# Router and experts of an adaLN block in plain float32 products instead of three-part bf16 ones; shared experts by feature rows, expert tiles written out, rows gathered by the index list in place

## The reference

```python
sa, ca, ga, sb, cb, gb = (silu(c) @ wmod) in six parts      # ga, gb pushed away from 0
h = layernorm(x) * (1 + ca) + sa
x = x + ga * attention(h)                                   # window of 8, softmax
h = layernorm(x) * (1 + cb) + sb
scores = sigmoid(h @ gate_w.T)                              # 2048 rows x 16 experts
topv, topi = top_k(scores, 2);  topv = topv / topv.sum()
y = mlp(h, sw1, sw2, sw3)                                   # shared, 352 wide
for e in range(16):                                         # 176 wide
    y = y + mlp(h, w1[e], w2[e], w3[e]) * weight of e for each row
x = x + gb * y
# mlp(x) = (silu(x @ w1.T) * (x @ w3.T)) @ w2.T; expert weights are bf16, h is float32
```

## Time and profile before

| | |
|---|---|
| median of 3 runs | 536.55 us (536.25 to 541.13) |
| profiled execution | 534.09 us |
| its span, first to last instruction | 532.3 us |
| mean granted TensorE clock | 0.914 |
| busy: TensorE, weight loads | 389.3 us (73%), 285.3 us (54%) |
| busy: VectorE, ScalarE, GpSimd | 311.2, 156.6, 169.8 us |
| chain that ended last | PE 52%, DVE 16%, issue 11%, unknown queue 8% |

### The profile page before, as it was taken

The page is one execution under the profiler, slowest core; times in us unless marked ns, Lnnn a source line. Parts: engine busy times, 40 slices in busy tenths (PEclk is TensorE's granted clock), DMA queues, the critical chain, the costliest instruction groups (busy, mean ns, idle before and its releaser), DMA issues.

```text
span 532.3 us, 14579 instructions
## 1 busy us (share of the span) xinstructions
PE 389.3 (73%) x5617; PEld 285.3 (54%) x5618; DVE 311.2 (58%) x704; ACT 156.6 (29%) x348; POOL 169.8 (32%) x164
## 2 busy tenths in 40 slices
PE   2779899998989898864877877765766576579200
PEld 0448687777868787643555655443544354346100
DVE  4736667775847575733979954444444445345283
ACT  1202041323222232214333223333333323334240
POOL 6100041222212230421000024545645555554362
PEclk9969999999999999986999989899898989987755
DMA  8440432314040314007300022222222322231392
GB/s 303 141 109 24 99 105 52 119 43 140 19 137 14 113 44 135 23 13 272 84 1 1 1 60 70 77 66 82 75 72 81 91 68 75 85 84 45 93 301 79
DMA packets 42313, 46.48 MB, mean 87 GB/s; under 512 B 21519, under 2 KB 36536, under 8 KB 42049
## 3 DMA queue, kind: packets, MB, share of 16 engines
q1 hardware_dynamic: 35491, 30.12, 18.7%
q0 software_dynamic: 5376, 13.65, 8.9%
q10 hardware_dynamic: 1398, 2.00, 1.1%
HBM read 32.03 MB, written 13.71 MB: 86 GB/s over the span
## 4 chain that ended last, share of the span: by engine, by line
PE 52%; DVE 16%; issue 11%; another core or an unknown queue 8%; ACT 4%; POOL 2%; DMA 2%; SPq 1%; DVEq 1%; POOLq 0%; ACTq 0%
PE bank L1246 9%; PE bank L1045 6%; PE bank L1072 6%; PE bank L1007 5%; PE bank L1054 3%; PE bank L1258 3%; PE bank L1060 2%; DVE second_region L927 2%; PE bank L1024 2%; PE bank L1159 2%; DVE hid L888 2%; PE bank L1089 2%; PE bank L1037 2%; ACT second_region L566 2%
## 5 line engine op out<-in xcount | busy, mean ns | idle before, releaser
L439 POOL DMA_INDIRECT second_region<-hrows,ixg x48 | 47.4, 989 | 139.0 <-DVE ixg L932 66.8
L1246 PE MATMUL bank<-region,second_region 128*128 x288 | 56.7, 337 | 25.5 <-DVE second_region L927 22.9
L888 DVE TENSOR_TENSOR hid<-second_region,bank 128x176 f32<-128x176 f32 (+1 forms) x64 | 24.4, 382 | 75.3 <-ACT second_region L566 62.2
L448 POOL DMA_INDIRECT yrows<-yo,ixp x48 | 50.8, 1059 | 19.6 <-issue 12.6
L1246 PEld LDWEIGHTS bank<-region,second_region 128*128 128x128 bf16 x288 | 27.4, 103 | 47.6 <-issue 36.2
L566 ACT ACTIVATE second_region<-bank 128x176 f32<-128x176 f32 (+1 forms) x64 | 22.5, 353 | 99.7 <-PE bank L1246 56.3
L1152 PE MATMUL bank<-cft,hid 128*88 128x128 f32 (+1 forms) x144 | 30.0, 304 | 29.7 <-DVE hid L888 28.4
L1258 PE MATMUL bank<-region,hT 88*128 x288 | 43.4, 291 | 1.1 <-DVE hT L902 1.0
L701 DVE RECIPROCAL second_region<-bank 128x256 f32<-128x256 f32 x16 | 28.1, 1758 | 26.2 <-PE bank L1077 26.2
L1045 PE MATMUL bank<-region,second_region 64*32 64x128 f32 x1024 | 38.4, 287 | 4.1 <-issue 4.1
L397 POOL TENSOR_TENSOR rstd2s<-ve,cft 128x2 f32<-128x2 f32 x8 | 5.5, 692 | 104.8 <-DVE ve L724 104.8
(11 more groups left out here) (150 smaller groups left out, 738.7 us busy)
## 6 DMA issues: line engine op xcount, KB each, us to landing
region<-vd SPq DMA_DIRECT2D x32, 128.0 KB, 3.2
modb<-moddram SPq DMA_DIRECT2D x8, 512.0 KB, 4.5
region<-yrows SPq DMA_DIRECT2D x16, 256.0 KB, 5.5
hrows<-h SPq DMA_DIRECT2D x8, 384.0 KB, 2.5
region<-w13T SPq DMA_DIRECT2D x1, 2816.0 KB
region<-second_region SPq DMA_DIRECT2D x64, 32.0 KB, 1.8
vd<-second_region SPq DMA_DIRECT2D x8, 256.0 KB, 2.2
out<-xs SPq DMA_DIRECT2D x8, 256.0 KB, 2.1
```

The source lines that it names most:

```text
L439: gp.indirect_dma_start(rows[:, j, :], None, hrows, bass.IndirectOffsetOnAxis(ap=ixg[:, j:j + 1], axis=0)).then_inc(fetch[j], 16)
L448: gp.indirect_dma_start(yrows, bass.IndirectOffsetOnAxis(ap=ixp[:, j:j + 1], axis=0), yo[:, j, :], None, bounds_check=TOPK * T - 1, oob_is ...
L888: dve.tensor_tensor(hid[:, j % 2, 0:w], act_s[:, j % 2, 0:w], bank[j % 2][:, boff:boff + w], ALU.mult).then_inc(hid_s, 1)
L1246: last = pe.matmul(bank[j % 2][:, 0:2 * I], rT[:, j % 2, q, :], w13[:, q % C, bass.ds(e, 1), :], start=q == 0, stop=q == PARTS * C - 1)
```

## The change

The products of router, shared experts and experts take float32 operands instead of three bf16 parts. h stays one float32 tile hx; hrows holds it in 1024 bytes a row. `modulated` on GpSimd is what is left of `split`; `turn_h` has 4 float32 transposes and `gate` 4 float32 products; ScalarE's `gate_exp` reads the scores from PSUM. In the tiles, hid's transposes are copied once (`turned_hidden`, to hT2), and `up` has 2, `down` 2 products, `turn_rows` 2 transposes.

The shared experts work on groups of four row tiles with the hidden features on the partitions: `up_shared` makes for 12 blocks (4 groups of 3) two products pairs of 512 columns, so that hid needs no transpose, and `down_shared` has 3 products a tile. The routing runs first for the 14 tiles that are ready, then for the last two (`rank` twice), and stands in another order between the shared blocks.

The weights must be float32 in SBUF: GpSimd loads sw13, sw2 and w2 at the start with a widening transfer; w13 is loaded in bf16 to a staging place, its first part in batch row 1 of the attention, and widened by eight copies on ScalarE (`widen`).

The 48 tiles are written out on all engines, with waits on constants; the transfers read their column of sloti directly, and ixg, ixp are gone. The buffers of the tiles lie where those of the shared experts lay, so the gathers wait for the last shared product (sy_p). The steps are in another order: `up` runs two tiles ahead (three PSUM places), `turn_rows` three; GpSimd's scatter is that of tile s, and stands behind the gather of s + 4.

The diff, cut to the tiles, the shared experts and the gate:

```diff
-            def split(b):
+            def modulated(b):
 
                 wait(gp, l2_xn, b + 1)
                 wait(gp, mod_ld, 16 * (b + 1))
                 gp.tensor_tensor(h2[:, :, :], h2[:, :, :],
-                                 modb[:, b, 2 * D:3 * D].unsqueeze(1).to_broadcast([P, U, D]), ALU.mult).then_inc(l2_mu, 1)
+                                 modb[:, b % 2, 2 * D:3 * D].unsqueeze(1).to_broadcast([P, U, D]), ALU.mult).then_inc(l2_mu, 1)
                 wait(gp, l2_mu, b + 1)
-                gp.tensor_tensor(h2[:, :, :], h2[:, :, :],
-                                 modb[:, b, D:2 * D].unsqueeze(1).to_broadcast([P, U, D]), ALU.add).then_inc(l2_h, 1)
-                wait(gp, p_hi, b + 1)
-                gp.tensor_tensor(hr[:, :, :], h2[:, :, :], h3[:, :, 0], ALU.subtract).then_inc(p_r, 1)
-
-            def last_part(b):
-                wait(gp, p_mid, b + 1)
...
-            gp.wait_ge(routed, 1)
-
-            def get(s, j, i):
+            gp.wait_ge(who_s, 2)
+            gp.wait_ge(sy_p, TT)
+
+            def get(s):
 
                 wait(gp, rT_p, s - RING + 1)
-                settle(gp)
-                wait(gp, ixg_s, s + 1)
-                settle(gp)
-                gp.indirect_dma_start(rows[:, j, :], None, hrows,
-                                      bass.IndirectOffsetOnAxis(ap=ixg[:, j:j + 1], axis=0)).then_inc(fetch[j], 16)
-
-            def give(s, j, i):
+                gp.indirect_dma_start(rows[:, s % RING, :], None, hrows,
+                                      bass.IndirectOffsetOnAxis(ap=sloti[:, 0, s:s + 1], axis=0)).then_inc(fetch[s % RING], 16)
+
+            def give(s):
 
                 wait(gp, yo_s, s + 1)
-                settle(gp)
-                wait(gp, ixp_s, s + 1)
-                settle(gp)
-                gp.indirect_dma_start(yrows, bass.IndirectOffsetOnAxis(ap=ixp[:, j:j + 1], axis=0),
-                                      yo[:, j, :], None, bounds_check=TOPK * T - 1,
-                                      oob_is_err=False).then_inc(put[j], 16)
-
-            def step(s, j, i):
-                if not (isinstance(s, int) and s + AHEAD >= NS):
-                    get(*later(i, j, AHEAD))
-                if not (isinstance(s, int) and s < 2):
-                    give(*later(i, j, -2))
-
-            for s in range(AHEAD):
-                get(s, s, 0)
-            over_tiles(gp, step, NS, RING)
-            for s in (NS - 2, NS - 1):
-                give(s, s % RING, s // RING)
+                gp.indirect_dma_start(yrows, bass.IndirectOffsetOnAxis(ap=sloti[:, 1, s:s + 1], axis=0),
+                                      yo[:, s % RING, :], None, bounds_check=TOPK * T - 1,
+                                      oob_is_err=False).then_inc(put[s % RING], 16)
+
+            for s in range(RING):
+                get(s)
+            for s in range(NS):
+                if s + RING < NS:
+                    get(s + RING)
+                give(s)
 
...
+            def silu(s):
+                wait(act, up_p, s + 1)
+                wait(act, hid_s, s - 1)
+                act.activation(act_s[:, s % 2, :], UP(s)[:, 0:I], ACT.Silu).then_inc(silu_s, 1)
+
+            def turned_hidden(s):
+                wait(act, ht_p, s + 1)
+                wait(act, y_p, s - 1)
+                act.activation(hT2[0:IH, s % 2], HT(s), ACT.Copy).then_inc(ht_s, 1)
+
+            def result(s):
+                wait(act, y_p, s + 1)
+                wait(act, put[s % RING], 16 * (s // RING))
+                act.activation(yo[:, s % RING, :], YP(s), ACT.Copy).then_inc(yo_s, 1)
+
+            silu(0)
+            silu(1)
+            for s in range(NS):
+                turned_hidden(s)
+                if s + 2 < NS:
+                    silu(s + 2)
+                if s > 0:
+                    result(s - 1)
+            result(NS - 1)
 
             for b in range(B):
                 act.wait_ge(ld_y[b], 16 * TOPK)
@@ -671,13 +665,6 @@
             for i, k in enumerate((2, 5)):
...
             def gate(b):
                 wait(pe, xT_s, b + 1)
                 if b == 0:
-                    pe.wait_ge(gw_s, 2 * PARTS - 1)
+                    pe.wait_ge(ld_g, 16)
                 for u in range(U):
-                    for q in range(PARTS * C):
-                        last = pe.matmul(LG[u], xT[:, U * b + u, q, :], gw3[:, q % C].rearrange("p k e -> p (k e)"),
-                                         start=q == 0, stop=q == PARTS * C - 1)
+                    t = U * b + u
+                    for c in range(C):
+                        last = pe.matmul(LG[:, u], xT[:, c, t * P:(t + 1) * P], gws[:, c, :], start=c == 0, stop=c == C - 1)
                 last.then_inc(lg_p, 1)
 
...
+            def up_shared(n):
+                g, f = divmod(n, SK)
+                p = SI - (SK - 1) * P if f == SK - 1 else P
+                wait(pe, su_m, n - 1)
+                for half, o in enumerate((SA(n), SB(n))):
+                    for c in range(C):
+                        last = pe.matmul(o[0:p], sw13[:, c, half * SI + f * P:half * SI + f * P + p],
+                                         xT[:, c, g * GT * P:(g + 1) * GT * P], start=c == 0, stop=c == C - 1)
+                last.then_inc(su_p, 1)
+
+            def down_shared(g):
+                wait(pe, su_m, SK * (g + 1))
+                for i in range(GT):
+                    wait(pe, sy_s, GT * g + i - 1)
+                    for f in range(SK):
+                        p = SI - (SK - 1) * P if f == SK - 1 else P
+                        last = pe.matmul(YP(i), hid_g[0:p, g % 2, f, i * P:(i + 1) * P], sw2[0:p, f, :],
+                                         start=f == 0, stop=f == SK - 1)
+                    last.then_inc(sy_p, 1)
+
+            def rank(a, z):
+
...
-            def turn_rows(s, j, i):
-                wait(pe, fetch[j], 16 * (i + 1))
-                wait(pe, rT_s, s - 1)
-                if isinstance(s, int) and s < 2:
-                    pe.wait_ge(hid_s, TT)
-                for q in range(PARTS * C):
-                    last = pe.transpose(RTP(j)[:, q * P:(q + 1) * P], rows[:, j, q * P:(q + 1) * P], identb)
+            down_shared(0)
+            up_shared(6)
+            down_shared(1)
+            up_shared(7)
+            up_shared(8)
+            sitters()
+            up_shared(9)
+            down_shared(2)
+            up_shared(10)
+            up_shared(11)
+            down_shared(3)
+
+            def turn_rows(s):
+                wait(pe, fetch[s % RING], 16 * (s // RING + 1))
+                wait(pe, rT_s, s)
+                for c in range(C):
+                    last = pe.transpose(RTP[:, c * P:(c + 1) * P], rows[:, s % RING, c * P:(c + 1) * P], ident)
                 last.then_inc(rT_p, 1)
 
-
-            held = [pe.alloc_register(f"expert_of_tile{k}") for k in range(RING + 2)]
-            experts = [None] * (RING + 2)
+            held = [pe.alloc_register(f"expert_of_tile{k}") for k in range(RING)]
+            later = [pe.alloc_register(f"expert_of_late_tile{k}") for k in range(RING)]
...
-            def down(s, j, e):
-                wait(pe, lo_s, TT + s + 1)
-                if isinstance(s, int) and s < 2:
-                    pe.wait_ge(y_s, TT + s - 1)
-                else:
-                    wait(pe, yo_s, s - 1)
+            def turn_hidden(s):
+                wait(pe, hid_s, s + 1)
+                wait(pe, ht_s, s - 1)
                 for k in range(2):
-                    for q in range(PARTS):
-                        last = pe.matmul(YP(j), hT3[0:IH, j % 2, q, k, :], w2[:, k, bass.ds(e, 1), :],
-                                         start=k == 0 and q == 0, stop=k == 1 and q == PARTS - 1)
+                    last = pe.transpose(HT(s)[:, k, :], hid[:, s % 2, k * IH:(k + 1) * IH], ident)
+                last.then_inc(ht_p, 1)
+
+            def down(s):
+                wait(pe, ht_s, s + 1)
+                wait(pe, yo_s, s - 1)
+                for k in range(2):
+                    last = pe.matmul(YP(s), hT2[0:IH, s % 2, k, :], w2[:, k, bass.ds(experts[s], 1), :],
+                                     start=k == 0, stop=k == 1)
                 last.then_inc(y_p, 1)
 
-            def step(s, j, i):
-                if j == 0 and not (isinstance(s, int) and s == 0):
-                    load_experts(i)
-                turn_hidden(TT + s, 2, IH, j)
-                if not (isinstance(s, int) and s + 1 == NS):
-                    up(s + 1, j + 1, experts[j + 2])
-                if not (isinstance(s, int) and s + 2 >= NS):
-                    turn_rows(*later(i, j, 2))
-                if not (isinstance(s, int) and s == 0):
-                    down(s - 1, j + 1, experts[j])
-
-            pe.wait_ge(ld_ew, 32)
-            pe.wait_ge(routed, 1)
-            turn_rows(0, 0, 0)
+            pe.wait_ge(su_m, SK * GROUPS)
+            pe.wait_ge(w_s, 8)
+            pe.wait_ge(ld_w2, 64)
+            pe.wait_ge(exp_s, 1)
```

(22 more changed lines are left out.)

675 lines of the change are left out of this document (298 added, 377 removed).

## The result

The changed kernel takes **601.2 us** (598.1 to 604.4, 4 runs), the kernel before beside it 536.4 (536.1 to 541.1): a ratio of 1.122, 95% interval 1.117 to 1.127. The forecast was 547 with a range of 505 to 582: the sign was right, the size was not, and the time lies outside the range. The profiled execution has a span of 602.6 us against 532.3, 70.3 more.

The account below looks back on a forecast made before the run. TensorE was taken to bound attention, no engine the shared stage, a chain of waits the tiles. Setup 2, attention 4.8, shared 1.7 and tiles 1.8 sum to +10.3: 544.4 by the profiled execution, 547 us by the median; range 505 to 582.

Parts of the forecast that it names:

- the ring: Expert tiles: product up, silu, result copy, scatter, gather, row transposes, next up wait in a circle; 7.7 us per two tiles.
- GpSimd's start: Expert tiles: GpSimd starts the scatter 0.24 us after ScalarE finishes the result copy.
- the gather's flight: Expert tiles: a gather takes 2.5 us from issue to landing, bounds 2.1 and 2.9.
- The clock: Expert tiles: 7.3 us for two tiles at full clock becomes 7.7 at this stretch's 0.92.
- Setup: 0 to 30 us: GpSimd's loads and weights flying beside qbd's spread cost +2 us, bounds 0 and 6.
- Attention: 30 to 232 us: float32 transposes and gate products on TensorE add 0.69 us a batch row, +4.8 us (0 to +8).
- Shared stage: Shared experts and routing: 85.6 us becomes 87.3 with TensorE's work, its stops and clock losses, +1.7 (-5 to +7).
- Rival 1: Expert tiles: the hold stays and lies in the ring, 30 us more, 577, or 607 if both tiles pay; chance 0.25.
- the hold: Expert tiles before the change: unexplained 2.92 us wait for another core or unknown queue, where gather and scatter stand together.
- Rival 2: Expert tiles: the ring doesn't close, TensorE bounds them at 129 + 4 us; 500 us; chance 0.20 with parts of it.
- Rival 3: Expert tiles: the loop itself caused the 1.4 us; written out it goes, 547 us, or 500 with Rival 2; no separate chance.
- The 1.4 us a tile: Expert tiles before the change: the mean tile's time beyond the 2.40 us between ups near the end, lying in waits.

Follow-up runs that it names:

- run with late loads: Changed kernel with GpSimd's six loads of sw13, sw2 and w2 moved from the setup to batch row 2 of the attention: 601.3 us.
- result ahead of silu: Changed kernel with ScalarE copying the result of tile s - 1 before the silu of tile s + 2: 554.6 us.
- opened ring: Changed kernel with GpSimd issuing the scatter of tile s - 2 instead of tile s behind the gather of s + 4: 493.6 us.
- written-out kernel: Kernel before the change with its three tile loops written out with constants, steps and order kept: 484.5 us.

## Why the prediction was wrong

**The step that failed is the length of the ring's turn.** The ring was put where it is: scatter ahead of gather, result behind silu, down, hid's transposes and up waiting behind the blocked row transposes. Of the 59.9 us between the forecast's +10.3 and the profiled +70.2, 53.4 are in the tiles. By its own terms (us, for two tiles):

| term | predicted | measured, turn shown |
|---|---|---|
| silu and result | 0.65 | 0.60 |
| until GpSimd starts | 0.24 | 0.80 |
| scatter and gap | 1.31 | 1.32 |
| gather to the row transposes | 2.6 | 2.93 |
| row transposes, down, hid's, up | 2.5, 2.9 with the clock | 4.42 |
| turn | 7.3, 7.7 with the clock | 10.07 |

21 turns of 2.4 us more are 50 of the 53. On the mean of the turns the gather's part is 3.2 us, which leaves 4.1 for the work behind it. So of the 50 us some 12 lie in GpSimd's start, 12 in the gather's flight and 26 in TensorE's work. (The 7.7 itself does not come out of its rows: with 0.92 on TensorE's 2.5 us alone the turn is 7.5, with 0.92 on all of it 7.9. Neither changes the account.)

- *The clock.* I scaled the turn by 0.92, the mean of a stage before in which TensorE hardly waited in one piece. In the ring all of TensorE's work on the path comes right behind a wait of 3 us, and takes 4.1 us on the mean where it takes 2.75 at full clock: 1.4 us a turn, 29 us over 21, of which I had 8. The mean of the stage after, 0.85, hides this too. Filling the wait brought the turn to 8.4.
- *GpSimd's start.* 0.24 was read from the earlier trace rows, where a gather starts 0.24 us behind the end of a result copy. But by the program a gather does not wait for a result. It waits for its index column, which VectorE copies:

```profile
343.69 1.01 POOL L448 DMA_INDIRECT yrows<-yo,ixp  x1 [0.30 <-PE bank L1224]
...
344.31 0.14 DVE L932 COPY ixg<-sloti 128x1 int32 x1
```

  The copy ends at 344.45 and the gather starts at 345.24, 0.79 us later, as it does at the three gathers before it (0.79 to 0.80); the scatter ahead of it ended at 344.70, 0.54 before. The releaser in brackets was a coincidence. In the changed kernel the scatter starts 0.80 to 0.84 us after the end of the result copy in all 25 places where it waited for one.
- *The gather's flight.* Taken from the scatter's 2.5, with bounds to 2.9; it is 2.7 / 2.8 / 3.9, and 3.2 on the mean of the 22 that stand in the chain. The estimate that the prediction worked out from the Trainium skill, DMA: Bandwidth & Descriptors, Anatomy of one DMA (2.3 us), was further off.

**Setup, +2, bounds to 6:** it is +6.9. The mechanism was right, the size over its upper bound; the loads of w2 do it. GpSimd's own issuing was priced too high (the six loads take 3.6 us of it in the run with late loads, not 6) and held nothing up.

**Attention, +4.8:** wrong in sign, -2.0, and within what repeats of one kernel show (198.0 to 204.1 for the versions of the changed one without loads in the attention, 201.4 to 207.0 for those of the kernel before). The gate's eight records cost 7.5 / 7 = 1.07 us a batch row and not 1.52, the transposes 0.61 and not 0.52; the rest of the price does not appear in the time, and what gives it back was not tried.

**Shared stage, +1.7, bounds to +7:** +9.4. The waits were as laid out: 5.6 for the one-hots, 4.9 at the down products, 2.0 for val. What was short is the work between them: the blocks take 47.2 us instead of 41.5, the downs 23.7 instead of 20.7, at a clock of 0.88. I had 3 us for this; it is 8.7. The same stage took 90.2 us in a profile in which its clock was 0.95 (result ahead of silu), so that some of it differs from run to run.

**Rival 1 (the hold stays and lies in the ring):** its 607 is the nearest number named, by the wrong cause. In the ring there is no hold: silu starts 0.02 us after its product, and no wait in the tiles is put down to "remote". **Rival 2 (the ring doesn't close):** not so, but it came near the tiles of the opened ring, 129 + 4 us against 128.6. **Rival 3 (the loop):** the loop costs nothing, shown by the written-out kernel (484.5 us against 484.6); the Trainium skill's rule on taken branches (Runtime: NRT & Kernel Launch, Instruction fetch mechanics) has no effect in this kernel that these runs could tell.

The 1.4 us a tile that I could not name came and went with the same code, so neither the order nor the loop alone makes it. Beside a kernel before without it the change costs 23% and not 12%.

## What to carry to other kernels

When a ring of waits is priced, price the work that stands right behind its wait at the lower clock, and count the start of the engine that is waked, not only the work of each. When a releaser stands in brackets, look in the program whether that instruction waits for it at all. And on a queue that fetches for later tiles and stores earlier ones, let the store lag far enough that its result is ready when its turn comes: this one line cost 107 of 601 us (78 where the hold takes its place).
